# Near path of 45 taps, corner points on the far list, far columns in batches of up to four

## The reference, cut to what matters

```
loc = ref + grid + offset / norm
samples = _bilinear_sample(img, 2 * loc - 1)
out = (samples * m).sum(-1)
out = out @ out_w + out_b
```

## Time and profile before

| what | value |
|---|---|
| median of 3 runs | 707.15 us |
| the profiled execution | 709.08 us, span 707.3 us |
| busy PE / DVE / ACT / POOL | 585.4 (83%) / 580.2 (82%) / 227.5 (32%) / 316.1 (45%) us |
| mean granted TensorE clock | 0.932 |
| instructions | 11117 |

### The profile page before, as it was taken

How to read it: one execution, slowest core, us unless ns; L and a number is a source line. 1 busy time by engine, 2 the same in 40 slices (tenths; PEclk the granted TensorE clock), 3 DMA queues, 4 the chain that set the end, 5 groups by cost and what they waited for, 6 DMA issues and landing times.

```text
span 707.3 us, 11117 instructions
## 1 busy us (share of the span) xinstructions
PE 585.4 (83%) x3456; PEld 432.8 (61%) x3456; DVE 580.2 (82%) x1052; ACT 227.5 (32%) x334; POOL 316.1 (45%) x326
## 2 busy tenths in 40 slices
PE   5992877888868869978888679889999999929995
PEld 3462655666546557556566567567777777715774
DVE  4579899999999999999999999836777766652766
ACT  6050600612413315206116000234454544413431
POOL 6523795797817796068278240201222211215111
PEclk8786998989999998999989799999999999977998
DMA  7057602003003006000000000000000000004011
GB/s 186 30 186 276 202 0 85 23 2 105 2 1 105 1 3 259 1 1 3 0 1 3 0 1 1 1 0 1 1 1 1 1 1 1 1 15 105 30 46 44
DMA packets 25594, 30.54 MB, mean 43 GB/s; under 512 B 5188, under 2 KB 17684, under 8 KB 25556
## 3 DMA queue, kind: packets, MB, share of 16 engines
q1 hardware_dynamic: 24654, 29.77, 12.8%
q0 software_dynamic: 896, 0.23, 0.4%
q10 hardware_dynamic: 6, 0.00, 0.0%
HBM read 24.94 MB, written 5.05 MB: 42 GB/s over the span
## 4 chain that ended last, share of the span: by engine, by line
PE 47%; DVE 25%; issue 13%; DVEq 2%; ACT 1%; POOL 0%; POOLq 0%; ACTq 0%
DVE prod L1391 11%; PE banks L797 10%; PE banks L912 8%; PE pair L892 8%; DVE stencil L1367 5%; DVE outer L1361 5%; PE pair L968 4%; PE banks L902 4%; PE banks L1002 4%; PE pair L750 3%; PE pair L743 2%; DVEq L1391 1%; PE banks L884 1%; PE banks L819 1%; PE banks L863 1%
## 5 line engine op out<-in xcount | busy, mean ns | idle before, releaser
L797 PE MATMUL banks<-ident,prod 128*128 128x128 f32 x1568 | 226.2, 291 | 79.5 <-DVE prod L1391 77.3
L797 PEld LDWEIGHTS banks<-ident,prod 128*128 128x128 f32 x1568 | 186.8, 149 | 139.5 <-DVE prod L1391 115.6
L1391 DVE TENSOR_TENSOR prod<-shifted,stencil 128x1024 f32 (+1 forms) x224 | 238.1, 1086 | 6.2 <-PE banks L797 6.2
L1187 POOL TENSOR_TENSOR rstd_now<-mv_now,neg_half 128x2 f32<-128x2 f32 x32 | 23.0, 718 | 131.6 <-DVE mv_now L1443 131.6
L750 PE MATMUL pair<-xg,dw_diag 128*128 128x512 f32 x144 | 73.9, 615 | 1.2 <-ACT dw_diag L514 1.2
L1159 POOL CAST far_list_i<-far_list 1x8 int32<-1x8 f32 x8 | 33.9, 4237 | 85.2 <-DVE far_list L1377 57.2
L912 PE MATMUL banks<-shifted 128*128 128x128 f32 x512 | 63.3, 277 | 2.3 <-ACT shifted L651 1.4
L912 PEld LDWEIGHTS banks<-shifted 128*128 128x128 f32 x512 | 60.2, 192 | 8.1 <-issue 6.1
L1361 DVE TENSOR_TENSOR outer<-hats 128x800 f32<-128x800 f32 x64 | 63.1, 987 | 0.8
L1367 DVE TENSOR_TENSOR stencil<-stencil,outer 128x800 f32 (+1 forms) x64 | 62.9, 983 | 0.3
L892 PE MATMUL pair<-shifted 128*128 128x512 f32 x128 | 61.0, 599 | 0.6 <-ACT shifted L634 0.6
(11 more groups left out here) (230 smaller groups left out, 849.0 us busy)
## 6 DMA issues: line engine op xcount, KB each, us to landing
shifted<-padded SPq DMA_DIRECT2D x42, 256.0 KB, 4.0
...
got<-padded,cell_now POOLq DMA_INDIRECT x28, 2.8
```

The costliest lines, as they stand in the source:

```text
L797: mm = pe.matmul(acc_of(c, r), prod[:, d % PROD, r * G:(r + 1) * G, :].rearrange("p g c -> p (g c)"), ident[:, :], is_transpose=True, star ...
L1391: ins = ve.tensor_tensor(prod[:, dx:dx + n, :, :], shifted[:, dx:dx + n, bass.ds(((c % HALF) * ROWS + dy) * G, ROWS * G), :], stencil_of[: ...
```

## The change: what it does

The window loses its 4 outermost corners: the near path has 45 taps (`NEAR`), listed in `TAP_AT` in the order of rows `ROW_ORDER`; rows 0 and 6 have 5 taps (two units of two, one of one), the other five keep 7. A chunk has 26 units. `prod` has a slot for each dx. A point that gives an outermost corner weight (both its offsets over 1 in size, outward, at a corner point of the 3 x 3) joins the far list; `corners` on DVE flags them from the hats. Offsets over 2 are flagged by ACT with two Sign activations that read PSUM behind the hats, in place of the square ahead of them; PE adds all flags in `count_far`. GpSimd takes up to four listed columns at once: `take` copies each column's operands into a lane, `cells` and `corner_weights` work on four lanes with one instruction, `gather` and `collect` run once a column. A cell is now weighed on the far path if it is over 2 from the point or an outermost corner of the window.

```diff
@@ -53,19 +53,23 @@
 GN_EPS = BN_EPS = LN_EPS = 1e-5
 GN_C = 4
-ROW_UNITS = -(-WIN // 2)
-UNITS = WIN * ROW_UNITS
+ROW_ORDER = (1, 0, 2, 3, 6, 4, 5)
+TAP_AT = [(dy, dx) for dy in ROW_ORDER for dx in range(WIN) if not (dy in (0, WIN - 1) and dx in (0, WIN - 1))]
+NEAR = len(TAP_AT)
+UNIT_AT = [(t, 2 if t + 1 < NEAR and TAP_AT[t + 1] == (dy, dx + 1) else 1)
+           for t, (dy, dx) in enumerate(TAP_AT) if (dx - (dy in (0, WIN - 1))) % 2 == 0]
+UNITS = len(UNIT_AT)
 BEGIN = 2
-AT_FAR, AT_CONV, AT_SAMPLES, AT_PROJECT = 18, 22, 35, 39
+AT_CONV, AT_FAR, AT_SAMPLES, AT_PROJECT = 16, 25, 31, 35
 AT_LIST = 5
-STENCIL_FILL = (0, 1, 1, 0, 1, 1, 0, 1, 1)
+STENCIL_FILL = (0, 1, 1, 0, 1, 0, 0, 1, 0)
 EXP_AT = 2
...
+MOST_CODE = int(FAR_UNIT) * (5 * P + 1) - 1
+BATCH = 4
...
 def first_of(unit):
-    return unit // ROW_UNITS * WIN + unit % ROW_UNITS * 2
+    return UNIT_AT[unit][0]
+def freed_by(tap):
+    dx = TAP_AT[tap][1]
+    before = [t for t in range(tap - NEAR, tap) if TAP_AT[t % NEAR][1] == dx]
+    return before[-1] + 1
...
-        off_most = sb("off_most", [P, ROWS * GP])
-        far = sb("far", [P, FAR_COLS], BF16)
+        signs = sb("signs", [P, 2, ROWS, 2 * GP], BF16)
+        at_corner = sb("at_corner", [P, ROWS * G, 2, 2], BF16)
+        far_unit = sb("far_unit", [P, 1], BF16)
...
                 sc.wait_ge(hats_used, k + 1)
-                sc.activation(far_xy, raw[:, :, 0:2 * GP], ACT.Square).then_inc(square_done, 1)
                 sc.wait_ge(off_done, k + 1)
...
+                if not isinstance(k, int) or k > 0:
+                    sc.wait_ge(far_mm, k)
+                    sc.sem_inc(act_waited, 1)
+                for i, sign in enumerate((1.0, -1.0)):
+                    last = sc.activation(signs[:, i, :, :], raw[:, :, 0:2 * GP], ACT.Sign,
+                                         bias=tap_bias[:, TAPS - 1:TAPS], scale=sign)
+                last.then_inc(signs_done, 1)
...
             def count_far(k):
-                pe.wait_ge(masks_done, k + 1)
+                pe.wait_ge(signs_done, k + 1)
+                pe.wait_ge(corners_done, k + 1)
                 if not isinstance(k, int) or k > 0:
                     pe.wait_ge(far_done, k)
                     pe.wait_ge(listed, k)
-                count = pair[1][:, 0:FAR_COLS]
-                pe.matmul(count, ones16[:, :], far[:, :], start=True, stop=False)
-                pe.matmul(count, ones[0:1, :], far_codes[:, :], start=False, stop=True).then_inc(far_mm, 1)
+                count = pair[1][0:1, 0:FAR_COLS]
+                by_corner = count.rearrange("p (g a b) -> p g a b", a=3, b=3)[:, :, 0:3:2, 0:3:2]
+                pe.matmul(count, ones[0:1, 0:1], far_codes[:, :], start=True, stop=False)
+                pe.matmul(by_corner, far_unit[:, :], at_corner[:, :, :, :], start=False, stop=False)
+                for i in range(4):
+                    mm = pe.matmul(count, far_unit[:, :], signs[:, i // 2, :, (i % 2) * GP:(i % 2 + 1) * GP],
+                                   start=False, stop=(i == 3))
+                mm.then_inc(far_mm, 1)
             def acc_of(c, r):
...
-                    c, d = k + i // STENCIL, i % STENCIL
-                    pe.wait_ge(prod_done, c * STENCIL + d + 1)
+                    c, t = k + i // NEAR, i % NEAR
+                    slot = TAP_AT[t][1]
+                    pe.wait_ge(prod_done, c * NEAR + t + 1)
                     for r in range(ROWS):
-                        mm = pe.matmul(acc_of(c, r), prod[:, d % PROD, r * G:(r + 1) * G, :].rearrange("p g c -> p (g c)"),
-                                       ident[:, :], is_transpose=True, start=(d == 0 and r == 0), stop=False)
+                        mm = pe.matmul(acc_of(c, r), prod[:, slot, r * G:(r + 1) * G, :].rearrange("p g c -> p (g c)"),
+                                       ident[:, :], is_transpose=True, start=(t == 0 and r == 0), stop=False)
                     mm.then_inc(prod_free, 1)
             def add_fix(k):
...
-                add_up(k, first_of(BEGIN), AT_FAR)
-                for i in range(AT_FAR, STENCIL):
+                add_up(k, first_of(BEGIN), AT_CONV)
+                for i in range(AT_CONV, NEAR):
                     if i == AT_FAR:
                         count_far(k + 1)
...
+            def take(k, row3, col, group, j):
                 slot = bass.ds(k % OFFS, 1)
                 xy = off[:, slot, :, :].rearrange("p s r (a o) -> p (s r a) o", o=GP)
                 here = place[:, :, :].rearrange("p r (a o) -> p (r a) o", o=GP)
+                now, middle = bass.ds(col, 1), bass.ds(group % G * PTS + PTS // 2, 1)
+                step(gp.tensor_copy(got_off[:, j, :], xy[:, bass.ds(row3, 3), now].rearrange("p a o -> p (a o)")), 1, False)
+                step(gp.tensor_copy(got_at[:, j, :], here[:, bass.ds(row3, 3), now].rearrange("p a o -> p (a o)")), 2, False)
+                step(gp.tensor_copy(got_mid[:, j, :], here[:, bass.ds(row3, 2), middle].rearrange("p a o -> p (a o)")),
+                     3, True)
+                gp.sem_clear(point)
+            def cells(n):
+                at, per = got_at[:, 0:n, 0:2], [P, n, 4]
+                step(gp.tensor_tensor(pos[:, 0:n, :], got_off[:, 0:n, 0:2], at, ALU.add), 1, True)
...
+                                      cell_c[:, 0:n].unsqueeze(2).to_broadcast(per), ALU.add), 7, True)
+                step(gp.tensor_copy(cell_now[:, 0:n, :], cell_f[:, 0:n, :]), 8, True)
+                gp.sem_clear(point)
+            def gather(j):
                 for a in range(4):
                     gp.indirect_dma_start(
+                        out=got[:, j, a, :], out_offset=None, in_=table,
+                        in_offset=bass.IndirectOffsetOnAxis(ap=cell_now[:, j, a:a + 1], axis=0)
+                    ).then_inc(gathered[j], 16)
+            def corner_weights(n):
+                near = [P, n, 2, 2]
+                step(gp.tensor_tensor(cell_at[:, 0:n, :], pos[:, 0:n, :], low[:, 0:n, :], ALU.subtract), 1, False)
+                step(gp.tensor_tensor(tap_d[:, 0, 0:n, :], low[:, 0:n, :], got_at[:, 0:n, 0:2], ALU.subtract), 2, False)
+                step(gp.tensor_tensor(tap_d[:, 1, 0:n, :], low[:, 0:n, :], got_mid[:, 0:n, :], ALU.subtract), 3, True)
...
+                step(gp.tensor_scalar(within, within, -1.0, 1.0, ALU.mult, ALU.add), 17, True)
+                step(gp.tensor_tensor(w_now[:, 0:n, :, :], w_now[:, 0:n, :, :], within, ALU.mult), 18, True)
+                gp.sem_clear(point)
+            def collect(k, group, j):
+                gp.wait_ge(gathered[j], 64)
+                gp.inc_swdge_sem([gathered[j]], [64], mode="sub")
+                w_flat = w_now[:, j, :, :].rearrange("p a b -> p (a b)")
+                step(gp.tensor_tensor(got[:, j, :, :], got[:, j, :, :], w_flat.unsqueeze(2).to_broadcast([P, 4, CG]),
+                                      ALU.mult), 1, True)
+                step(gp.tensor_tensor(got_sum[:, :, :], got[:, j, 0:2, :], got[:, j, 2:4, :], ALU.add), 2, True)
+                step(gp.tensor_tensor(got_sum[:, 0, :], got_sum[:, 0, :], got_sum[:, 1, :], ALU.add), 3, True)
                 to = fix[:, bass.ds(k, 1), bass.ds(group, 1), :].rearrange("p s a c -> p (s a c)")
+                step(gp.tensor_tensor(to, to, got_sum[:, 0, :], ALU.add), 4, True)
                 gp.sem_clear(point)
+            def add_batch(k, j0, n):
+                codes = [gp.value_load(far_list_i[0:1, j0 + j:j0 + j + 1], min_val=0, max_val=MOST_CODE) for j in range(n)]
+                groups = [(code // GROUP_UNIT) % (ROWS * G) for code in codes]
+                for j in range(n):
+                    with gp.If(codes[j] > int(FAR_UNIT) - 1):
+                        take(k, (codes[j] // (G * GROUP_UNIT)) % ROWS * 3,
+                             (codes[j] % GROUP_UNIT).with_bounds(min_val=0, max_val=GP - 1), groups[j], j)
+                    gp.nop()
+                cells(n)
+                for j in range(n):
+                    with gp.If(codes[j] > int(FAR_UNIT) - 1):
+                        gather(j)
+                    gp.nop()
+                corner_weights(n)
+                for j in range(n):
+                    with gp.If(codes[j] > int(FAR_UNIT) - 1):
+                        collect(k, groups[j], j)
+                    gp.nop()
...
                 with gp.Else():
-                    with gp.Fori(0, LIST - 1) as j:
-                        code = gp.value_load(far_list_i[0:1, bass.ds(j, 1)], min_val=0, max_val=int(FAR_UNIT) * (P + 1) - 1)
-                        with gp.If(code > int(FAR_UNIT) - 1):
-                            add_point(k, (code // (G * GROUP_UNIT)) % ROWS * 3, (code % GROUP_UNIT).with_bounds(min_val=0, max_val=GP - 1),
-                                      (code // GROUP_UNIT) % (ROWS * G))
+                    for j0 in range(0, LIST - 1, BATCH):
+                        some = gp.value_load(far_list_i[0:1, j0:j0 + 1], min_val=0, max_val=MOST_CODE)
```

(34 more changed lines are left out.)

139 lines of the change are left out of this document (70 added, 69 removed).

## The result

| | before | after |
|---|---|---|
| median of 9 runs each | 708.83 us | 712.17 us |
| the profiled execution | 709.08, span 707.3 | 715.7, span 713.9 |
| first turn's start / last product's end | 68.36 / 447.85 | 68.84 / 452.22 |
| columns on GpSimd, gathers | 7, 28 | 11, 44 |

The ratio of the runs is 1.0067, 95% interval 1.0043 to 1.0091: slower by 4.7 us (3.3 by the medians), where 14 were forecast. The profiled execution of the changed kernel is 3.5 us over its median, the one before 0.2 over its own, so differences of a few us between these two profiles aren't all the change's. The direction held and the size did not. The two parts of the sum, -4 for the turns and +18 for GpSimd's lag, were both wrong, in opposite directions.

A forecast was written before the change was run, and what follows sets the result against it. DVE was taken to set the pace from 68 to 448 us. Turns at -4 us and GpSimd's stalls at +18 make +14, so 721 us against 707.15; likeliest range 708 to 728, chance 0.50.

The forecast's parts named there:

- -4 for the turns: Chunk loop: seven turns give -1.5 us, chunk 7's products -2.3, the stencil ahead of the first turn -0.5.
- +18 for GpSimd's lag: DVE's listing of far columns waits for late GpSimd iterations: stalls of 3, 7.5 and 7.5 us, 18 in all.
- the hats wait: DVE idles 1.7 us ahead of weigh_hats for ACT's hats, which end 16.35 us after T, the start of finish_silu.
- The rest of a turn: From weigh_hats to the turn's end: 35.75 us before, loses 2.3, gains 0.5, becomes 33.95.
- GpSimd keeps up: Rival: GpSimd's iterations 0 to 3 end within 238 us, no stall is left, 703 us; chance 0.17.
- a factor of 1.1: GpSimd's iterations: multiplier on quiet costs for longer waits, taken between 1 and the 1.24 seen before the change.
- the quiet sum: GpSimd's iteration cost in a quiet stretch: 32.7 us once plus 14.3 a column, ahead of the multiplier.
- a further tap of slot wait: Bound on the turns: DVE's wait for PE's slot grows by one more tap, making the turns' sum -1 us.
- 7 x 1.55: First part of each of seven turns, up to weigh_hats: grows from 14.9 to 16.45 us, logits done 1.55 later.
- dependent start, 0.1 each: DVE's stencil: two more zeros in STENCIL_FILL each lay bare a dependent start, 0.1 us each.
- the hats wait doesn't show, while GpSimd lags: Rival: ACT or PE comes earlier, turns 2.5 us shorter, stalls about as much longer, 707 us; chance 0.12.
- both: Rival: no hats wait and no GpSimd lag, DVE's whole saving of 25 us arrives, 682 us; chance 0.07.

The follow-up runs named there:

- run 1: The changed kernel with EXP_AT = 4, so ACT takes the softmax's exp behind the fourth hat instead of the second: 709.86 us, ratio 1.0008.
- Run 7: The changed kernel without the product that puts corner points on the far list, 7 far columns in place of 11: 713.46 us, ratio 1.0073.
- Run 13: The changed kernel with only the stencil's last filler unit moved from behind its eighth point to behind its ninth: 709.35 us, ratio 1.0008.
- Run 14: The kernel before, with a filler unit moved so that nothing stands between the stencil's last sum and the next chunk's first product: 718.24 us, ratio 1.0133.
- Run 6: The changed kernel with exp behind the fourth hat and without the product that lists corner points, 7 far columns for 11: 704.47 us, ratio 0.9965.
- run 12: The changed kernel with later exp and fix, more buffers for far counts and list, the last filler moved, idle TensorE transposes: 702.10 us, ratio 0.9908.
- run 2: The changed kernel with ROW_ORDER = (1, 2, 0, 3, 6, 4, 5), a row of 5 taps third instead of second: 711.79 us, ratio 1.0047.
- run 8: The changed kernel with its 11 far columns handled one at a time in place of batches of up to four: 768.5 us, ratio 1.0874.

## Why the prediction was off

**Right.** The counts of products, gathers and columns; the prices of DVE's instructions; PE's slots (T+4.82 for 4.75), exp (T+9.8 for 9.7) and the hats wait (T+16.5 for 16.45) in the turns at full clock; the rest of a turn at 33.8 to 34.5 us (33.95 forecast); a batch that gives nothing for one column. That the total came out slower, as forecast, is in part luck: the 18 us that were to make it slower did not come, and the 4 us that were to be saved turned into a loss.

**The term that failed most: GpSimd's 18 us.** The step was "Iteration 1, three columns: 207.3, so a stall of 3 ... Iteration 2: ... a stall of 7.5. Iteration 3 the same". The stalls were 0: MAX8 never waited for GpSimd, which was one of the forecast's own signs of being wrong. Iterations 0 to 3 took 52.8 (with its first cast, 58 charged), 66.1, 52.9 and 59.5 us where 52, 83, 67 and 67 were charged; from the first cast they needed 233.7 us, under the 238 which the rival "GpSimd keeps up" named as its point. That rival had the stalls right and the time wrong (703), since it shared the -4. The prediction knew both prices of a small instruction, 0.9 beside DVE's work and 0.20 without, and took 0.9 for nearly all, with a factor of 1.1 on top that came from the kernel before. In iteration 1 the factor's 7.6 us did not come; of the quiet sum of 75.6 us the copies took 6.2 for the 11.7 charged with their registers, the cells 3.3 for 7.6 and the weights 13.9 for 16, while the gathers took 23.3 for 19.2. The same prediction had put 1.7 us of hats wait into each turn, and that wait is where the cells ran fast; run 1, without it, shows them slow again and the stalls there. Run 7 shows that in the changed kernel the columns cost nothing. The forecast's mechanism was real, and the changed kernel lies just on the other side of the point from which it counts.

Two smaller steps of the text don't hold as they stand. DVE's product at 175.25 was read as one "with GpSimd at work", but what GpSimd did then was to issue gathers; that small instructions don't slow DVE is shown by run 7. And a further tap of slot wait, 0.6 us in seven turns, takes the -4 to about 0, not to -1.

**The term of the other sign: -4 us for the turns.** From the first turn to the last product it became +3.9 (383.4 us against 379.5). In the bullets, the first part of a turn ends and the rest begins at `weigh_hats`.
- The first parts of the turns together grew by 14.3 us where 7 x 1.55 = 10.9 were charged. In turns 1 and 5, at full clock before and after, the charge was right (1.65 and 1.59); turns 2, 3 and 6 came 1.1 to 1.6 us later, by the low clock at their start, of which the forecast has no term. Turn 0 began at the low clock in both kernels.
- The rest of six turns shrank by 7.3 us where 6 x 1.8 = 10.8 were credited. The turn that I took as the model, at 169.99, was the longest of them: 35.75 us where the six have 35.27 in the mean; its MAX8 came 0.3 to 0.5 us later behind `weigh_hats` than in the others. One turn was read as if it were all.
- Within that rest, the "dependent start, 0.1 each" was 0.5 us at the stencil's end.
- The rest of turn 6 with chunk 7 shrank by 3.1 us where 4.1 were credited.

Run 13 shows that one filler unit is behind the 0.5 us and behind the late starts of turns 2, 3 and 6, though one in turn 1 came in their place: with it moved, the stretch from the first turn to the last product is 378.6 us, 0.9 less than before the change. Run 14 shows that such a gap costs 9 us in the kernel before too, about half of it by a stall for GpSimd.

Run 1 is the rival "the hats wait doesn't show, while GpSimd lags": 709.9 us where it had 707. Run 6 takes both limits away and is at 704.5, not at the 682 of the rival "both": about 1.3 us of slot wait in the turns at full clock, the wait for the stencil and four low-clock starts are still in it.

**Left open.** In the profiled execution the last stage took 261.7 us against 259.4, though the change doesn't touch it. That is 2.2 of the 6.6 us between the two profiles. It differs in the profiles of all variants, from 258.9 (run 12) to 262.9 (run 2), and 269.2 in run 8; the runs don't settle what sets it. Nor do they settle why a gap of the same length brings the low clock in one turn and not in another.
